# An attention and stencil kernel on one core: transposes of the probabilities and the projection ahead of the second QKV product

## What is computed

```python
x = x + L0(_gn(x))          # _gn: normalisation over 32 groups of 6 channels
x = x + L1(_gn(x))
# L0: windows of N = 64 pixels, NH = 6 heads of HD = 32
v  = einsum('bchw,oc->bohw', x, V_w) + V_b
qk = einsum('bchw,oc->bohw', x, QK_w) + QK_b
o = irfft2(rfft2(qp) * rfft2(kp), s=(8, 8))
attn = softmax(einsum('bhnd,bhmd->bhnm', o, vv) + bias)
y = einsum('bhnm,bhmd->bhnd', attn, vv)
return einsum('bchw,oc->bohw', y, proj_w) + proj_b
# L1
out = x + depthwise_laplacian(x)
return conv1x1(out, merge_w) + merge_b
```

## Time and profile before

| | |
|---|---|
| median of 3 runs | 5577.6 us (5576.49 to 5582.28) |
| profiled execution, its own time | 5581.64 us |
| its span, first to last instruction | 5579.7 us |
| mean granted TensorE clock | 0.995 |
| busy: PE, DVE, ACT, POOL | 5356.6 us (96%), 4229.7 (76%), 3757.7 (67%), 4099.7 (73%) |
| HBM traffic | 96 GB/s over the span |

### The profile page before, as it was taken

One profiled execution on the slowest core, in us unless ns is written; L12 is line 12 of the kernel. 1 busy time (PEld: TensorE's weight loads), 2 busy tenths in 40 slices (PEclk: granted clock), 3 DMA queues, 4 the chain that ended last, 5 costly groups with the idle time before them and its releaser, 6 DMA issues.

```text
span 5579.7 us, 207720 instructions
## 1 busy us (share of the span) xinstructions
PE 5356.6 (96%) x90620; PEld 4638.2 (83%) x90620; DVE 4229.7 (76%) x6658; ACT 3757.7 (67%) x7653; POOL 4099.7 (73%) x3518
## 2 busy tenths in 40 slices
PE   7999999999999999999999999999999999999988
PEld 5888788888888888888888888888888888888865
DVE  5777677777777777787777877777777777777758
ACT  3666776667766677667676677666776677766643
POOL 1555557887887777878878777778778788787864
PEclk9999999999999999999999999999999999999989
DMA  4221123333333333432333333333333323233336
GB/s 139 63 74 55 51 74 106 113 93 94 109 111 108 88 105 103 115 107 84 104 113 108 104 85 107 114 106 99 93 107 111 113 85 88 81 85 86 87 98 181
DMA packets 392507, 550.39 MB, mean 99 GB/s; under 512 B 24822, under 2 KB 284729, under 8 KB 391610
## 3 DMA queue, kind: packets, MB, share of 16 engines
q1 hardware_dynamic: 391612, 537.11, 33.6%
HBM read 335.69 MB, written 201.33 MB: 96 GB/s over the span
## 4 chain that ended last, share of the span: by engine, by line
PE 67%; ACT 15%; POOL 12%; issue 3%; DVE 1%; DMA 1%; SPq 1%; POOLq 0%; ACTq 0%; DVEq 0%
PE b_q L576 18%; PE b_q L657 7%; PE b_t L671 6%; PE b_t L647 6%; PE b_s L689 5%; ACT probsT L970 3%; PE b_t L629 3%; ACT probs L1115 3%; PE b_s L524 3%; PE b_s L537 2%; PE b_s L526 2%; POOL yl L1251 2%; PE b_s L535 2%; POOL yb L1253 2%; PE b_s L585 2%
## 5 line engine op out<-in xcount | busy, mean ns | idle before, releaser
L1246 POOL TENSOR_TENSOR probs<-probs,srec 128x768 f32<-128x768 f32 x512 | 818.8, 1599 | 684.7 <-DVE srec L953 684.7
L909 DVE TENSOR_TENSOR probs<-b_s,posb 128x768 f32<-128x768 f32 x512 | 490.3, 958 | 675.9 <-PE b_s L689 673.9
L903 DVE TENSOR_TENSOR qkl<-b_q,qkh 128x384 fp32r<-128x384 f32 x1024 | 570.8, 557 | 514.7 <-ACT qkh L970 481.8
L970 ACT ACTIVATE vs<-b_q 128x192 f32<-128x192 f32 x1024 | 338.7, 331 | 784.1 <-PE b_q L576 784.1
L1225 POOL TENSOR_TENSOR probs<-probs,smax 128x768 f32<-128x768 f32 x512 | 755.0, 1475 | 57.2 <-DVE smax L914 17.8
L1251 POOL TENSOR_TENSOR yl<-yT,yh 128x256 fp32r<-128x256 f32 x512 | 376.0, 734 | 460.9 <-ACT yb L970 460.9
L576 PE MATMUL b_q<-wnh,xh 128*128 128x288 f32 x2048 | 670.4, 327 | 10.2 <-DVE qkl L903 7.1
L1161 POOL TENSOR_TENSOR dg<-late 128x645 f32<-128x645 f32 x352 | 563.0, 1599 | 68.1 <-DMA late<-x_dram 45.6
L970 ACT ACTIVATE qkh<-b_q 128x384 fp32r<-128x384 f32 x1024 | 497.7, 486 | 170.5 <-PE b_q L576 170.5
L576 PE MATMUL b_q<-wnl,xhl 128*128 128x288 f32 x2048 | 605.5, 296 | 0.0
L576 PE MATMUL b_q<-wnl,xh 128*128 128x288 f32 x2048 | 604.8, 295 | 0.0
(11 more groups left out here) (194 smaller groups left out, 15658.2 us busy)
## 6 DMA issues: line engine op xcount, KB each, us to landing
ld<-in_x SPq DMA_DIRECT2D x192, 512.0 KB, 4.6
late<-x_dram SPq DMA_DIRECT2D x112, 640.0 KB, 5.0
xs<-in_x SPq DMA_DIRECT2D x128, 512.0 KB, 4.0
x_dram<-late SPq DMA_DIRECT2D x128, 512.0 KB, 2.7
out<-late SPq DMA_DIRECT2D x128, 512.0 KB, 2.8
late<-x_dram SPq DMA_DIRECT2D x240, 192.0 KB, 5.5
xs<-in_x SPq DMA_DIRECT2D x128, 256.0 KB, 4.5
x_dram<-late SPq DMA_DIRECT2D x128, 256.0 KB, 3.5
```

Of the source, the lines that this page charges most:

```text
L903: V.tensor_tensor(qkl[:, i % 2, :], q_out, qkh[:, i % 2, :].bitcast(F32), ALU.subtract).then_inc(lo_out, 1)
L909: V.tensor_tensor(scored(i).rearrange("p (t q) m -> p t q m", q=4), scores.rearrange("p (t q m) -> p t q m", q=4, m=N), posb[:, :, :].unsq ...
L970: return A.activation(o, i, ACT.Copy)
L1246: P.tensor_tensor(probs[:, i % 2, :, :], probs[:, i % 2, :, :], srec[:, i % 2, :].unsqueeze(2).broadcast_to([128, 12, N]), ALU.mult).then_ ...
```

## The change

On PE the six transposes of the probabilities move from behind the transposes of v to a place behind `m_slot(2j)`, and both halves of the projection follow them, ahead of `qkv(2j+1)`. On ACT the copy of probsT moves ahead of the second copy of v, and the exponential behind the copy of vT; the small steps `weights` and `border` move behind it. On DVE the product of the transforms and the first `remainders` come ahead of the maximum. In the setup `group_mean`, `group_spread` and the biases stand at other steps of the position bias. In the last blocks `source_load` goes ahead of `result_store` on SP.

```diff
@@ SP, per block
                 double_started(4 * blk + 2)
+                v = blk - STENCIL_LAG + 1
+                if 4 * blk >= DOUBLES and 0 <= v < STRIPS:
+                    source_load(v)
                 v = blk - MERGE_LAG - 1
                 if 0 <= v < STRIPS:
                     result_store(v)
...
-                if 0 <= v < STRIPS:
+                if 4 * blk < DOUBLES and 0 <= v < STRIPS:
                     source_load(v)
@@ PE, setup
             for m in range(N):
-                if m == 56:
+                if m == 38:
                     group_mean(0)
-                elif m == 58:
+                elif m == 41:
                     group_spread(0)
-                elif m == 60:
+                elif m == 57:
                     bias(0, 0)
...
+                if m == 61:
+                    pe.wait_ge(m_read, 3)
+                    bias(0, 1)
...
             last.then_inc(pos_mm, 1)
-            pe.wait_ge(m_read, 3)
-            bias(0, 1)
@@ PE, main loop
                 m_slot(2 * j, pair)
+                if pair(3):
+                    k, n = pair(3)
+                    pe.wait_ge(norm_done, n)
+                    if pair(1):
+                        pe.wait_ge(prod_done, pair(1)[1])
+                    for i in range(2):
+                        for t in range(3):
+                            last = nc.tensor.transpose(
...
+                    last.then_inc(pT_mm, 1)
                 if pair(4):
...
                     project(b_r[:, 0:256], 0, n)
+                    project(b_r[:, 256:512], CB, n).then_inc(proj_mm, 1)
                 if pair(0):
...
                     nc.tensor.transpose(vt_out[0:CB, 2, :], vs[:, at, CA:C], ident[:, :]).then_inc(vT_mm, 1)
-                if pair(3):
-                    k, n = pair(3)
-                    pe.wait_ge(norm_done, n)
...
-                    last.then_inc(pT_mm, 1)
-                if pair(4):
-                    project(b_r[:, 256:512], CB, pair(4)[1]).then_inc(proj_mm, 1)
                 m_slot(2 * j + 1, pair)
@@ DVE, main loop
-                    dve.wait_ge(s_out, n)
-                    V.tensor_reduce(smax[:, i % 2, :], scored(i), AX.X, ALU.max).then_inc(max_done, 1)
-                if pair(0):
-                    remainders(2 * j)
                 if pair(1):
...
                                     ALU.mult).then_inc(prod_done, 1)
+                if pair(0):
+                    remainders(2 * j)
+                if pair(2):
+                    i, n = pair(2)
+                    dve.wait_ge(s_out, n)
+                    V.tensor_reduce(smax[:, i % 2, :], scored(i), AX.X, ALU.max).then_inc(max_done, 1)
                 statistics(2 * j)
@@ ACT, main loop
                 split(h, 0 if j % 2 == 0 else 2)
-                weights(blk, ph)
-                if ph == 0 and 0 <= blk - STENCIL_LAG < STRIPS:
-                    border(blk - STENCIL_LAG)
+                if pair(3):
+                    act.wait_ge(pT_mm, pair(3)[1])
+                    copy(probsT[:, :, :, :].rearrange("p i h n -> p i (h n)"), q_banks[:, 0:2, 0:6 * N]
+                         ).then_inc(pT_out, 1)
                 if pair(0):
                     v_copy(2 * j + 1)
+                if pair(0):
+                    high(2 * j + 1)
+                    act.wait_ge(vT_mm, pair(0)[1])
+                    copy(vT[:, j % 2, :, :], vt_out).then_inc(vT_out, 1)
                 if pair(2):
...
                     A.activation(pr, pr, ACT.Exp).then_inc(exp_done, 1)
-                if pair(0):
-                    high(2 * j + 1)
...
-                if pair(3):
-                    act.wait_ge(pT_mm, pair(3)[1])
...
+                weights(blk, ph)
+                if ph == 0 and 0 <= blk - STENCIL_LAG < STRIPS:
+                    border(blk - STENCIL_LAG)
                 a_result(2 * j + 1)
```

More of the change, by code:

```diff
@@ L621, in _ @@
                     nc.tensor.transpose(vt_out[0:CB, 2, :], vs[:, at, CA:C], ident[:, :]).then_inc(vT_mm, 1)
-                if pair(3):
-                    k, n = pair(3)
-                    pe.wait_ge(norm_done, n)
-                    if pair(1) and not pair(0):
-                        pe.wait_ge(prod_done, pair(1)[1])
-                    for i in range(2):
-                        for t in range(3):
-                            last = nc.tensor.transpose(
-                                q_banks[:, i, t * 128:(t + 1) * 128],
-                                probs[:, k % 2, 4 * t + 2 * i:4 * t + 2 * i + 2, :].rearrange("p w m -> p (w m)"),
-                                ident[:, :])
-                    last.then_inc(pT_mm, 1)
-                if pair(4):
-                    project(b_r[:, 256:512], CB, pair(4)[1]).then_inc(proj_mm, 1)
                 m_slot(2 * j + 1, pair)
@@ L1115, in _ @@
                     A.activation(pr, pr, ACT.Exp).then_inc(exp_done, 1)
-                if pair(0):
-                    high(2 * j + 1)
-                    act.wait_ge(vT_mm, pair(0)[1])
-                    copy(vT[:, j % 2, :, :], vt_out).then_inc(vT_out, 1)
-                if pair(3):
-                    act.wait_ge(pT_mm, pair(3)[1])
-                    copy(probsT[:, :, :, :].rearrange("p i h n -> p i (h n)"), q_banks[:, 0:2, 0:6 * N]
-                         ).then_inc(pT_out, 1)
+                weights(blk, ph)
+                if ph == 0 and 0 <= blk - STENCIL_LAG < STRIPS:
+                    border(blk - STENCIL_LAG)
                 a_result(2 * j + 1)
```

3 lines of the change are left out of this document (added).

## The result

| | before | after |
|---|---|---|
| median, same chip | 5577.05 us (5573.07 to 5582.28, 4 runs) | 6013.18 us (6012.14 to 6015.34, 4 runs) |
| span of the profiled execution | 5579.7 us | 6010.4 us |
| PE busy, granted clock | 96%, 0.995 | 90%, 0.993 |
| first score addition | 108.13 us | 100.91 us |
| the next 76 doubles | 756.3 us | 803.0 us |

The ratio is 1.078, 95% interval 1.077 to 1.080: slower, as forecast, but by 436 us and not by 323, and 23 us above the range. The last four lines are differences between starts of the score addition (L909 before, L912 after) in DVE's timeline. They add up to the 430.7 us between the spans: -7.2, +46.7, +400.8, -9.6.

What follows compares the result with a forecast made beforehand. PE, busy 96%, bounds the kernel, in a ring of four engines waiting for each other. Main doubles +292, rare slots +28, first 78 doubles +10, setup -7: +323 on 5581.6, about 5900 us (1.058); range 5725 to 5990.

Steps and rivals of the forecast that it cites:

- The row sum is late: On DVE, row sum L935 starts 7.12 or 7.39 us after score addition L909 starts (L), instead of 5.60: 1.5 to 1.8 late.
- The meeting of xhl and POOL: Odd doubles: xhl on DVE waits for POOL's last neighbour subtraction, ends 0.55 after it; 11.52 us, or 10.80 without L723.
- The rival without the meeting: Second rival: in odd doubles xhl starts ahead of POOL's subtraction; +123 instead of +292, 5730 us; 0.2 including a mixture at 5815.
- X - P (1.84): On PE, from the start of the probabilities' transposes (P) to the second QKV (X): transposes 0.58, projection halves 0.67 and 0.59.
- even doubles, 10.65 forecast: Iterations ending through L820 on DVE: row sum at 7.12, then 2.48, 0.06 and 0.99, 10.65 us in all.
- An even double after that starts late on DVE, so P is limited by DVE.: The probabilities' transposes on PE (P) wait for DVE's product, L + 1.88, not for PE's own work, L + 2.15.
- the rare slots: Bias and means slots in the main loop: half of 0.26 us per pair disappears in PE's idle time, half stays, +28 us.
- the first 76 doubles, +10 forecast: First 78 doubles in the prediction, no pieces or stencil: 10.01 even and 10.42 odd against 10.08 now, +10 us.
- this queue position of the exponential does [cost]: On ACT the exponential behind vT's copy starts at L + 6.24 or later; the later maximum costs nothing of its own.
- The third rival: POOL takes over: the projection waits for yb if odd doubles last less than 10.8; 21.0 per pair, 5670 us; chance 0.03.
- The sign of being wrong by the clock: The prediction fails if PE's granted clock, expected still near 1.00, falls in the new gaps.
- The first rival: Faster: row sum's lateness fits under DVE's slack, below 1.1 us in even doubles; 5455 or 5515 us; chance 0.04.

Runs made afterwards that it cites:

- experiment 5: Changed kernel with x1 moved on DVE from behind the row sum to ahead of the second qkl; 5789.13 us, 1.038.
- experiment 2: Changed kernel with the stencil's last subtraction on POOL done for one row instead of four; 5906.69 us, 1.059.
- experiment 9: Changed kernel with DVE's old order (maximum, remainders, then product), PE and ACT keeping the new one; 6693.63 us, 1.201.
- Experiment 3: Changed kernel with ACT's small steps weights and border back ahead of the copy of probsT; 6006.86 us, 1.077.
- experiment 4: Kernel before with only the earlier group steps in the setup and the earlier source_load in the last blocks; 5561.65 us, 0.9972.
- experiment 1: Changed kernel with the exponential on ACT back ahead of the second qkh and vT; 5905.75 us, 1.059.
- experiment 10: Changed kernel with the second half of the projection on PE back behind the transposes of v; 5743.45 us, 1.030.
- experiment 11: Changed kernel with x1 and xhl ahead of the row sum on DVE and POOL's diagonal ahead of its subtraction of the maximum; 5719.49 us, 1.026.

## Why the prediction was right in its sign and short in its size

**Right.** The row sum is late by what was put ahead of the second QKV and by the exponential's new place: L + 7.14 to 7.26 at three places of four and 7.61 at the fourth, against 7.12 or 7.39 in the forecast, and the exponential releases it in every double. What stood behind it on DVE then set the time; experiment 5, which moves only x1 out of that queue, takes back 224 us. The meeting of xhl and POOL was forecast at 1.53 and an end 0.55 behind POOL's, and measured 1.52 (1.16 at j % 4 = 3, where it starts later) and 0.55; odd doubles of 11.52 and 10.80 were measured as 11.53 and 10.81. The Trainium skill's rule that the second to start waits for all of the first (page "SBUF — State Buffer", section "SBUF: two separate sides") agrees with these rows: xhl's end followed L1179's end by 0.55 and 0.54, though it had started 0.21 and 0.57 behind it. The rival without the meeting would have been 170 us away; experiment 2 puts the meeting at 106. The setup (-7) was -7.2. X - P (1.84) was 1.83 to 1.85.

**Short: even doubles, 10.65 forecast, 11.00 and 10.89 measured, +40 us over 137 pairs with L726.** By terms, for j % 4 = 0, medians of the changed trace: P - L 2.16 instead of 1.88, X - P 1.85, X to row sum 3.26 instead of 3.40, row sum to L823's end 2.49, then 0.26 instead of 0.06 to the scores, and 0.98; the sum is 11.00. Two terms failed.
- "An even double after that starts late on DVE, so P is limited by DVE." The product was ready, but PE was not: ahead of P stands the piece, and the piece's slot waits for the score addition (`m_slot` waits for s_out). The piece takes 0.94 and starts 0.26 behind L912's end at j % 4 = 0, which gives P = L + 2.16, and 0.15 behind it at j % 4 = 2, which gives L + 2.05. I counted PE's work from S and left this wait out of the sum, though the description of the kernel before names it and the prediction expects PE to be seen waiting there. In the profile before PE shows no idle time at it.
- The signal from L823 to the scores was taken as 0.06, and no row of the kernel before shows it, because the scores come 1.1 later there. In the changed trace it is 0.26. The signal from the product to P was taken as 0.07 in the same way and is 0.15 where it counts, in the first doubles and in experiment 9.

Without L726 the forecast pair was 21.89 and the measured one is 22.02: the even double takes 11.21 and not 11.09. Over 79 pairs this is 10 us.

**Short: the rare slots.** Half of today's 56 us was to disappear in PE's new idle time and half to stay (+28). Main sum: forecast 4479.6 + 320 = 4800, measured 4880.4, 81 more. By the medians of the table the plain doubles make 52 of them (40 and 10 as above, 2 in odd doubles); 9 are that plain doubles before were shorter than the 20.46 per pair that was read from one block. The other 20 are the rare slots: what the doubles have above their medians was 59 us before and is 51 after, 8 less and not 28. The idea that idle time hides them held for most of them (51 to 22 us) and failed for one: the double of 15.7 to 17.3 once in an image, 6 of them in this stretch, has 28 us above its median where it had 8. The step that failed there is that such a slot can itself stand in the chain: mn comes late from ACT, PE's slot waits 3.73 for it, and everything behind it in the ring waits too. Experiment 3 shows that putting it back ahead of the exponential gives the same sum.

**Short: the first 76 doubles, +10 forecast, +46.7 measured.** 10 us of it is a misreading of the earlier trace rows: the window from 90 us on holds 18 us of setup ahead of the first L909 at 108.13, so these doubles took 9.95 before (756.3 / 76) and not 10.08, and the forecast doubles (10.01 and 10.42) mean +20. The medians are 10.18 and 10.54 (the row sum is at L + 7.08, the scores 0.25 behind x1's end, not 0.06), 11 us; one double of the long kind adds 6, and slots of 0.3 to 1 us each the last 10.

**Counted at nothing, a gain:** the earlier source_load, 9.6 us here at the end and 11 in experiment 4.

**A step that the result alone doesn't test:** "this queue position of the exponential does [cost]". It was partly true. With the exponential back (experiment 1) the row sum starts at L + 6.8, not at the 5.6 of before, so its place makes 0.45 of the 1.7 us of lateness, worth 107 us. Half the projection behind the second QKV again brings 0.59 and 270 us (experiment 10). The larger part of the lateness is the second QKV's place.

**The third rival** (POOL takes over) didn't rule the time, but its mechanism is real: it wanted odd doubles under 10.8, and where experiments 1, 5 and 10 bring them to 10.3 to 10.5, PE waits for yb 60, 73 and 114 times (twice in the changed kernel).

**The sign of being wrong by the clock** was seen only in part: the mean granted clock stays at 0.993, and it falls in the one large gap of an image (experiment 3).

**The first rival** (faster) needed lateness under 1.1 us; experiment 11 shows that it would have failed even with this ring open: 5719 us, with PE waiting 168.7 us for vT.

## What to carry to other kernels

- Work moved ahead of something on the busiest engine delays everything that is behind it, on the other engines too. Follow every instruction that needs the delayed result, and then every queue that such an instruction stands in. Here the exponential, qkh, qkl and the row sum stand one behind another on two engines.
- Work out a shortened loop for every engine and for every place in the pattern. With the exponential put back the row sum came 0.45 earlier as worked out, but 107 of 280 us came of it: one odd double of two still met POOL, and behind the other one POOL became the late engine.
- When a wait must be late, look at what stands behind it without needing it. Moving x1 past the late row sum gave 224 us, moving xhl 110, and moving xhl in the old kernel 0.3%.
- In a chain of waits, count the waits of every instruction that stands ahead of the one you time, also those that never showed in the old profile because something else was later. And check what else lies in a window before dividing its length by a count: 18 us of setup cost this forecast 10 us.

## What the runs showed of the hardware

- The wait between DVE and POOL goes in both directions and can pass on. In the changed kernel L1179 holds xhl back (1.52 or 1.16 instead of 0.69), and L1251 starts 0.93 behind xhl and takes 1.93 instead of 1.47; its end is 1.34 behind xhl's.
- A table load on ACT took 1.283 us in all 32 loads of the changed kernel, 15 of them at the exponential's line, one after each square root. With the pair of loads in two doubles (changed kernel) or ahead of one exponential (experiment 3) the total was the same.
- From DVE's end to PE's start it is 0.15 in some waits (L912 to the piece at j % 4 = 2, xhl to the QKV product, the product to P) and 0.26 in others (L912 to the piece at j % 4 = 0, L823 to the scores), in the median. Why they differ wasn't tried.
- PE's granted clock fell to its lower level (0.50, 1.2 GHz) in 58 of the first 76 doubles of experiment 9, where PE waits for the product 2.15 us per double on average, and in one of these 76 in the changed kernel, where it waits 0.6. In the main stretch of experiment 9, where it waits 1.1, the mean granted clock is 1.00.
